# The first normalization and query projection are moved into the opening of the wide attention

## What is computed

```python
x = x + _L0_xattn_ref(_layernorm(x, axis=-1), ctx_1024, L0_xattn_ln_gamma, L0_xattn_ln_beta, L0_xattn_w_q, L0_xattn_w_kv, ...)

def _L0_xattn_ref(x, context, ln_gamma, ln_beta, w_q, w_kv, w_out, b_out, gate):
    xn = _layernorm(x, ln_gamma, ln_beta)
    q = (xn @ w_q).reshape(B, SQ, NUM_HEADS, DIM_HEAD)
    kv = context @ w_kv
    k, v = jnp.split(kv, 2, axis=-1)
    ...
    scores = jnp.einsum('bhqd,bhkd->bhqk', q * SCALE, k)
    attn = jax.nn.softmax(scores, axis=-1)
    out = jnp.einsum('bhqk,bhkd->bqhd', attn, v).reshape(B, SQ, INNER)
```

## Time and profile before

| | |
|---|---|
| median of 3 runs (lowest, highest) | 3983.5 us (3973.45, 3986.92) |
| profiled execution | 3982.38 us, its span 3980.6 us |
| busy share of the span | PE 89%, DVE 63%, ACT 58%, POOL 42% |
| mean granted TensorE clock | 0.951 |
| the part that the change touches | the first 118 us or so |

### The profile page before, as it was taken

One profiled execution on the slowest core, in us unless ns is written; L12 is line 12 of the kernel. 1 busy time (PEld: TensorE's weight loads), 2 busy tenths in 40 slices (PEclk: granted clock), 3 DMA queues, 4 the chain that ended last, 5 costly groups with the idle time before them and its releaser, 6 DMA issues. The chain is left out here.

```text
span 3980.6 us, 81241 instructions
## 1 busy us (share of the span) xinstructions
PE 3557.9 (89%) x30262; PEld 2604.8 (65%) x30262; DVE 2489.8 (63%) x3852; ACT 2289.7 (58%) x4298; POOL 1657.8 (42%) x1365
## 2 busy tenths in 40 slices
PE   6899999999999999999787976799999977679399
PEld 4687788778787788887546974455555543344398
DVE  5666666666666666664274113678788777468687
ACT  3666666666666766666252112466666666536265
POOL 0587777777777777777232002110111000014043
PEclk9999999999999999999888997799999999779699
DMA  6677767776777676665103656878787754100011
GB/s 241 253 291 285 260 257 278 275 278 249 277 276 267 249 276 240 240 240 186 42 8 132 242 216 216 191 175 168 180 168 181 137 74 65 26 15 2 20 46 43
DMA packets 231412, 723.00 MB, mean 182 GB/s; under 512 B 47324, under 2 KB 128220, under 8 KB 162140
## 3 DMA queue, kind: packets, MB, share of 16 engines
q1 hardware_dynamic: 228336, 709.44, 56.3%
q0 software_dynamic: 2688, 8.39, 0.6%
HBM read 623.47 MB, written 94.24 MB: 180 GB/s over the span
## 5 line engine op out<-in xcount | busy, mean ns | idle before, releaser
L805 POOL TENSOR_TENSOR wa_acc<-wa_acc,wa_probs 128x512 f32<-128x512 f32 x960 | 1256.9, 1309 | 460.5 <-ACT wa_probs L650 352.1
L715 DVE TENSOR_REDUCE wa_mx<-wa_ps_x 128x1 f32<-128x512 f32 x1024 | 658.6, 685 | 361.5 <-PE wa_ps_x L503 361.4
L650 ACT ACTIVATE wa_probs<-wa_ps_s 128x512 f32<-128x512 f32 x1024 | 530.4, 602 | 548.8 <-PE wa_ps_s L546 548.3
L1444 DVE TENSOR_REDUCE na_mx<-na_ps_m 128x2 f32<-128x1024 f32 x512 | 613.8, 1220 | 202.1 <-PE na_ps_m L1265 198.6
L1389 ACT ACTIVATE na_probs<-na_ps_s 128x512 f32<-128x512 f32 x1024 | 555.9, 594 | 317.5 <-PE na_ps_s L1285 315.1
L642 ACT ACTIVATE wa_ps_s<-wa_m_wide 128x512 f32<-128x512 f32 x1024 | 578.5, 614 | 0.0
L524 PE MATMUL wa_ps_o<-wa_probs,wa_values 128*64 128x256 f32 x4096 | 468.7, 381 | 0.0
L524 PEld LDWEIGHTS wa_ps_o<-wa_probs,wa_values 128*64 128x64 f32 x4096 | 285.6, 137 | 158.5 <-ACT wa_probs L650 23.9
L468 PE MATMUL wa_ps_x<-w_k_ctx,wa_w_k 128*128 128x512 f32 x1488 | 380.9, 403 | 7.7 <-DMA w_k_ctx<-ctx_split 7.3
L491 PE MATMUL wa_ps_x<-wa_w_v,w_v_ctx 128*128 128x256 f32 x2880 | 363.8, 283 | 0.1
L491 PEld LDWEIGHTS wa_ps_x<-wa_w_v,w_v_ctx 128*128 128x128 f32 x2880 | 356.9, 191 | 6.4 <-issue 0.5
(11 more groups left out here) (399 smaller groups left out, 5745.2 us busy)
## 6 DMA issues: line engine op xcount, KB each, us to landing
w_k_ctx<-ctx_split SPq DMA_DIRECT2D x248, 1024.0 KB, 6.9
w_v_ctx<-ctx_split SPq DMA_DIRECT2D x120, 1024.0 KB, 8.1
na_keys<-k_rows SPq DMA_DIRECT2D x384, 128.0 KB
na_ctx<-ctx_split SPq DMA_DIRECT2D x43, 1024.0 KB, 11.7
ctx_split<-w_stage SPq DMA_DIRECT2D x32, 1024.0 KB, 5.0
first_keep<-in_ctxT SPq DMA_DIRECT2D x32, 512.0 KB, 11.2
ge_w_b<-in_w_rows SPq DMA_DIRECT2D x8, 2048.0 KB, 7.9
k_rows<-na_k_high SPq DMA_DIRECT2D x64, 256.0 KB, 2.8
```

What stands on the lines that cost most here:

```text
L650: act.activation(probs[:, c % R:c % R + 2, h * SQ:(h + 1) * SQ], ps_s[n % BANKS][:, :].rearrange("p (c n) -> p c n", c=2), ACT.Exp).then_i ...
L715: dve.tensor_reduce(mx[:, half, h, k:k + 1], ps_x[banks[h]][:, :], AX.X, ALU.max).then_inc(m_taken, 1)
L805: pool.tensor_tensor(to[:, :], to[:, :], probs[:, c % R, :], ALU.add).then_inc(summed, 1)
L1444: dve.tensor_reduce(mx[:, half, :, k], ps_m[n % 2][:, :, :], AX.X, ALU.max).then_inc(m_taken, 1)
```

## The change

The block of the query projection disappears; its work is put into the wide block, in every engine's list.

- Loads: `x`, `ident`, the first context piece, the first weights, the second context piece, `ones`. The block still ends when `x`, `ident` and `ones` have landed. Gamma, beta and `wq` are loaded by the wide block.
- Room: `wq` lies in the last 8 chunks of `values`, the normalized rows `xn` and their transpose `xT` in `probs`, the full keys in `acc`, the queries' high and low parts on their way out in `v_ctx`. So values 6 and 7 must wait until the projection is over.
- TensorE: blocks 0 to 3 (`EARLY` = 4), then the 8 rows are turned, units 0 and 1, blocks 4 and 5, keys 6 and 7, then the 16 maxima with units 2 to 15 between them, then values 6 and 7.
- VectorE: the two normalizations, gamma and beta, units' low parts, the maxima. GpSimd takes over the low parts of the context, of the first weights and of the keys, and reads the keys from a full copy that ScalarE makes (`k_full`). ScalarE also copies the values. The units' scaled copy is gone: the high part is taken from PSUM with the scale, the low part by one `scalar_tensor_tensor`.
- SP: `store(4)` and what follows stand behind the stores of units 0 and 1 and `queries(0)`; the other units' stores stand behind `store(7)` and two context loads.

The diff, cut to its core (new semaphores, the unchanged arithmetic of `normalize`, and the passing of arguments are left out):

```diff
...
+        k_full = acc
...
+        pt, pq = [ps_o, ps_x[1]], ps_s[2:4]
...
+        UNITS = 2 * PAIRS
+        EARLY = 4
+        def unit_at(i):
+            return i + 2 if i + 2 < UNITS else None
...
+            def store_queries(n):
+                rows, cols = slice(n // 2 * P, (n // 2 + 1) * P), slice(n % 2 * 512, (n % 2 + 1) * 512)
+                sp.wait_ge(q_high_ready, n + 1)
+                sp.dma_start(q_high[rows, cols], q_stage[0][n % 2].bitcast(F32)).then_inc(q_out[n % 2], 16)
+                sp.wait_ge(q_low_ready, n + 1)
+                sp.dma_start(q_low[rows, cols], q_stage[1][n % 2].bitcast(F32)).then_inc(q_out[n % 2], 16)
+            sp.dma_start(gb[:, 0, :], gamma.partition_broadcast(P)).then_inc(affine_in, 16)
+            sp.dma_start(gb[:, 1, :], beta.partition_broadcast(P)).then_inc(affine_in, 16)
+            sp.dma_start(wq, w_q.rearrange("(k p) n -> p k n", p=P)).then_inc(wq_in, 16)
+            for k in range(EARLY):
+                fetch(k + 2)
+                store(k)
+            fetch(EARLY + 2)
+            store_queries(0)
+            store_queries(1)
+            sp.wait_ge(q_out[0], 32)
             queries(0)
-            for k in range(CG):
-                if k + 2 < CG + 2:
-                    fetch(k + 2)
-                store(k)
-                if k == 3:
+            store(EARLY)
+            fetch(EARLY + 3)
+            store(EARLY + 1)
+            fetch(EARLY + 4)
+            fetch(EARLY + 5)
+            store(CG - 2)
+            store(CG - 1)
+            key_context(CG)
+            key_context(CG + 1)
+            for n in range(2, UNITS):
+                store_queries(n)
+                if n == 3:
+                    sp.wait_ge(q_out[0], 64)
                     queries(1)
+                if n == 5:
+                    sp.wait_ge(q_out[0], 96)
+                    queries(2)
+                if n == 9:
                     key_weights(1)
-                if k == 5:
-                    key_context(CG)
-                if k == 6:
-                    key_context(CG + 1)
             key_weights(2)
-            queries(2)
+            for i in range(2):
+                sp.wait_ge(q_out[i], 16 * UNITS)
...
-                        pe.wait_ge(kl_ready, k)
+                        pe.wait_ge(kh_ready, k)
+                        pe.wait_ge(k_full_ready, k)
...
+            def project_unit(n):
+                if n >= 2:
+                    pe.wait_ge(q_high_ready, n - 1)
+                    pe.wait_ge(q_low_ready, n - 1)
+                for k in range(KD):
+                    ins = pe.matmul(pq[n % 2][:, :], wq[:, k, n // 2 * P:(n // 2 + 1) * P], xT[:, k, n % 2 * 512:(n % 2 + 1) * 512],
+                                    start=(k == 0), stop=(k == KD - 1))
+                ins.then_inc(q_done, 1)
+            def first_values(k):
+                for hb in (2 * k, 2 * k + 1):
+                    project_values(0, hb, ps_s[hb % 2])
+            for k in range(EARLY):
                 project_keys(k, ps_x[2])
-                project_values(0, 2 * k, ps_s[2 * k % BANKS])
-                if k:
-                    first_maximum(k - 1, 0)
-                project_values(0, 2 * k + 1, ps_s[(2 * k + 1) % BANKS])
-                if k:
-                    first_maximum(k - 1, 1)
-            first_maximum(CG - 1, 0)
-            first_maximum(CG - 1, 1)
+                first_values(k)
+            for t in range(NT):
+                turn_row(t)
+            pe.wait_ge(wq_in, 16)
+            pe.wait_ge(evacuated, NT)
+            project_unit(0)
+            project_unit(1)
+            for k in range(EARLY, CG):
+                project_keys(k, ps_x[2])
+                if k < CG - 2:
+                    first_values(k)
+            for i in range(2 * CG):
+                first_maximum(*divmod(i, 2))
+                if unit_at(i) is not None:
+                    project_unit(unit_at(i))
+            pe.wait_ge(q_low_ready, UNITS)
+            first_values(CG - 2)
+            first_values(CG - 1)
...
+            def root(n):
+                act.wait_ge(inv_ready, n + 1)
+                act.activation(rstd, inv, ACT.Sqrt).then_inc(root_ready, 1)
+            def first_keys(k):
+                take_keys(k, ps_x[2])
+                if k >= 2:
+                    act.wait_ge(kl_ready, k - 1)
+                act.activation(k_full[k % 2][:, :], ps_x[2][:, :], ACT.Copy).then_inc(k_full_ready, 1)
+            def first_values(k):
+                for hb in (2 * k, 2 * k + 1):
+                    act.wait_ge(vproj_done, hb + 1)
+                    act.activation(values[:, 2 * hb:2 * hb + 2, :], ps_s[hb % 2][:, :].rearrange("p (c n) -> p c n", c=2), ACT.Copy
+                                   ).then_inc(v_ready, 1)
...
+            def unit_high(n):
+                act.wait_ge(q_done, n + 1)
+                if n >= 2:
+                    act.wait_ge(q_out[n % 2], 32 * (n // 2))
+                act.activation(q_stage[0][n % 2], pq[n % 2][:, :], ACT.Copy, scale=Q_SCALE).then_inc(q_high_ready, 1)
+            act.activation(warm, ident[:, 0:1], ACT.Sqrt)
             split(0)
+            first_weights()
             split(1)
-            for k in range(CG):
-                take_keys(k, ps_x[2])
-                if k + 2 < CG:
+            root(0)
+            for k in range(EARLY):
+                first_keys(k)
+                first_values(k)
+                if k == 1:
+                    root(1)
+                split(k + 2)
+            for t in range(NT):
+                take_row(t)
+            unit_high(0)
+            unit_high(1)
+            for k in range(EARLY, CG):
+                first_keys(k)
+                if k < CG - 2:
+                    first_values(k)
                     split(k + 2)
+            for i in range(2 * CG):
+                if unit_at(i) is not None:
+                    unit_high(unit_at(i))
+            first_values(CG - 2)
+            first_values(CG - 1)
...
+            def normalize(n):
...
+            def unit_low(n):
+                dve.wait_ge(q_high_ready, n + 1)
+                dve.scalar_tensor_tensor(q_stage[1][n % 2], pq[n % 2][:, :], Q_SCALE, q_stage[0][n % 2].bitcast(F32),
+                                         ALU.mult, ALU.subtract).then_inc(q_low_ready, 1)
+            normalize(0)
+            normalize(1)
+            scale_rows()
+            unit_low(0)
+            unit_low(1)
+            for i in range(2 * CG):
+                take_maximum(0, *divmod(i, 2), (0, 1))
+                if unit_at(i) is not None:
+                    unit_low(unit_at(i))
...
+            def first_weights(n, to, land):
+                pool.wait_ge(first_high, n + 1)
+                pool.tensor_tensor(to[:, 1, :, :], land[:, :, :], to[:, 0, :, :].bitcast(F32), ALU.subtract).then_inc(first_ready, 1)
+            def split_low(n):
+                pool.wait_ge(high_ready, n + 1)
+                if n >= 2:
+                    pool.wait_ge(stored[n % 2], 16 * (n // 2))
+                pool.tensor_tensor(stage[n % 2][:, 1, :, :], land[n % 2], stage[n % 2][:, 0, :, :].bitcast(F32), ALU.subtract
+                                   ).then_inc(low_ready, 1)
+            def first_keys(k):
...
+                pool.wait_ge(k_full_ready, k + 1)
+                pool.tensor_tensor(keys_low[0][:, cols], k_full[k % 2][:, :], keys_high[0][:, cols].bitcast(F32), ALU.subtract
+                                   ).then_inc(kl_ready, 1)
+            split_low(0)
+            first_weights(0, w_k[0], k_land)
+            first_weights(1, w_v, v_land)
+            split_low(1)
             pool.wait_ge(first_ready, 2)
             load_weights(0)
+            for k in range(CG):
+                first_keys(k)
+                if k + 2 < CG:
+                    split_low(k + 2)
...
+            with nc.Block() as block:
+                @block.sync
+                def _(sp):
...
+                    sp.dma_start(x[:, :, :], x_rows).then_inc(loaded, 16)
+                    sp.dma_start(ident[:, :], a["ident"]).then_inc(loaded, 16)
+                    sp.dma_start(land0[0], a["ctxT"][0:1, :, 0:512].rearrange("o (k p) n -> p (o k) n", p=P)).then_inc(land_in[0], 16)
+                    sp.dma_start(k_land[:, :, :], w_kv[:, 0:P].rearrange("(k p) n -> p k n", p=P)).then_inc(first_in, 16)
+                    sp.dma_start(v_land[:, :, :], w_kv[:, PAIRS * P:(PAIRS + 2) * P].rearrange("(k p) n -> p k n", p=P)
+                                 ).then_inc(first_in, 16)
+                    sp.dma_start(land0[1], a["ctxT"][0:1, :, 512:1024].rearrange("o (k p) n -> p (o k) n", p=P)).then_inc(land_in[1], 16)
+                    sp.dma_start(ones[:, :], a["ones"]).then_inc(loaded, 16)
+                    sp.wait_ge(loaded, 48)
```

(20 more changed lines are left out.)

104 lines of the change are left out of this document (54 added, 50 removed).

## The result

The change makes no difference that counts, and what it makes is a loss: median 3989.9 us over 20 runs (3983.4 to 4002.7) against 3980.4 over 20 of the kernel before (3972.1 to 3987.7, and one slow execution of 6700 us, which has no part in the ratio). The ratio is 1.0024, 95% interval 1.0017 to 1.0032, so +9.6 us (6.8 to 12.7). The forecast was 3986, +2.3; the measured time is in its range and, but for the end of the interval, within the 0.3% called no change.

A forecast was written before the change was run, and what follows sets the result against it. TensorE and DMA are both nearly full in the opening's last big stage. `open_banks` at 120.9 against 117.4, less 1.2 for keys 8 and 9, gives +2.3 us on 3982.4; with 1.1 for the median, 3986, range 3972 to 3999.

The forecast's parts named there:

- the shared port: VectorE and GpSimd side by side in the opening: holding each other costed at nothing, with 5.6 us of cover.
- Blocks 0 to 3: First context blocks of the opening: TensorE starts at 17.2 us, 5.7 a block, block 3 ends at 38.0.
- rival 1: VectorE and GpSimd block each other in the opening: second root asked for at 28.5, +3 to +5 us, 3990; chance 0.12.
- Rows and first units: Eight rows behind `split(5)` at about 0.4 us each, to 45.4; units 0 and 1 take 3.45 and 1.7, to 50.7.
- Keys 6 and 7: Behind blocks 4 and 5: `store(4)` goes out at 53.8, TensorE waits 2.6 us, keys 7 end at 69.0.
- The burst: DMA traffic from 67 us: 5.5 million bytes take 15 us at 369 GB/s; unit 4 taken at 82.5, stall of 6.
- Restart and units: Units beside the maxima behind the stall: chain of 2.5 us a unit, unit 15 done at 109.6, maxima to 112.8.
- Rival 3: Faster opening: TensorE stays the bound, stores land in 5.0, chain hides; 99.5 for 117.4, so 3966; chance 0.12.
- The end: Values 6 and 7 behind the units: 6.4, copy 0.8, clock 0.8, to 120.9; keys 8 and 9 give back 1.2.
- in TensorE's terms: Count of TensorE's opening: starts 12.3 us earlier, 16 of old gaps go; new 4.5, 5, 13, 3 and 3.
- Rival 2: Units' stores in the opening land in 5.5 us, not 2.0: 3.6 a unit against 2.5, so 4001; chance 0.18.
- Rival 4: Partly faster opening: short landings -4, half the burst's stall -3, units at 2.3 -2, so 3977; chance 0.13.

The follow-up runs named there:

- E3: Changed kernel with the eight turned rows taken by ScalarE ahead of `split(5)`; ratio 1.0015 to the kernel before, landmark 125.51 for 131.63.
- E2: Changed kernel with `store(4)`, `fetch(7)` and `store(5)` issued ahead of the stores of units 0 and 1; ratio 1.0018 to the kernel before, landmark 129.26.
- E1: Changed kernel with the two 1 MB context loads issued behind unit 7's stores; ratio 1.0016 to the kernel before, landmark 131.82.
- E4: Changed kernel with the stores of units 2 to 15 issued from GpSimd's queue, `split_weights(1)` behind unit 9's; ratio 1.0028 to the kernel before, landmark 134.06.
- E5: Changed kernel with four buffers instead of two for the queries' high and low parts; 3984.1 us, landmark 129.22.
- E8: Changed kernel with E1, E2, E3, E5 and E6 together; median 3973.1 us, ratio 0.9980 to the kernel before, landmark 116.71.
- E9: E8 with the two context loads right behind `store(5)`; median 3971.8 us, ratio 0.9964 to the kernel before, landmark 111.06.
- E11: Changed kernel with the two context loads issued behind `fetch(6)`; median 3981.1 us, ratio 0.9991 to the kernel before, landmark 126.51.
- E6: Changed kernel with VectorE reducing each maximum before it makes the next unit's low part; 3990.3 us, landmark 128.79.
- E7: Changed kernel with gamma and beta left out of the first normalization, so its result lacks them; 3978.9 us, landmark 131.24.
- E10: E9 with the low parts of context blocks 6 and 7 made by VectorE; median 3971.0 us, ratio 0.9967 to the kernel before, landmark 119.64.

## Why the prediction was nearly right, and what in it was off

**The whole.** Direction, band and the order of the waits held; the sum was +2.3 for a measured +8.5 at the landmark. No rival's time came true for its reason. What was wrong are sizes, and nearly all on one side; and one term that was put at nothing, the shared port, was not nothing.

| step | forecast | measured |
|---|---|---|
| first statistics; first keys | 11.3; 17.2 | 10.94; 16.60 |
| VectorE asks for the second root | 23.2 | 29.0 |
| block 3 ends | 38.0 | 37.5 |
| norm ends; block 4's low part ends | 37.9; 39.0 | 41.2; 43.4 |
| last row taken | 45.4 | 47.1 |
| units 0 and 1 done | 50.7 | 52.97 |
| keys 6; keys 7 start | 62.9; 66.8 | 65.15; 69.22 |
| first maximum | 69.0 | 72.05 |
| `unit_high(4)` | 82.5 | 87.67 |
| a unit | 2.5 | 2.51 |
| values 6 start | 112.8 | 119.66 |
| `open_banks` | 120.9 | 127.85 |

**Blocks 0 to 3** came out on TensorE as forecast, within 0.6: GpSimd's subtraction 1024 wide, forecast 2.55 from the one 512 wide, has a median of 2.355. Beside them VectorE's norm and the low part of block 4 were 3.3 and 4.4 us late, which was covered here (see rival 1).

**Rows and first units: +2.3 us.** `split(5)` at 41.0 was seen (41.69), and E3 shows it to be the gate. But a row cost 0.61, not 0.4: turning and copying wait for each other, and the clock column is 0.65 there. I had taken the low clock for unit 0 alone. Units 0 and 1 took 5.7 for 5.15.

**Keys 6 and 7: +0.1 in the wait, +0.7 in the clock.** `store(4)` was forecast at 53.8 and issued at 56.33, late by 2.5, of which 2.3 are the units'; E2 confirms the mechanism. The second keys ran for 2.90 where 2.2 were put.

**The burst: +2.1 us.** From the first maximum to `unit_high(4)` I had 13.5 and it was 15.6. The 369 GB/s were fair (422 and 361 in two windows); the bytes weren't. Units 2 and 3 put 1.05 million of their own in before unit 4 could go, 2.7 us at 391 GB/s, and I had counted only what stood ahead of them. Over 69.2 to 87.65 us, from the start of the burst to unit 4, DMA moved 355 GB/s, that is 6.55 million bytes, the 5.5 of the forecast and these 1.05. E1, E4, E5, E8, E9 and E11 show that bytes in this stretch are the main cost, not places in a queue. The prediction's words, that unit 2's stores are "behind them" in the queue, suggest that a reordering helps; E1 and E4 refute that.

**Restart and units: +1.7 us.** 2.51 a unit was met, and E6 shows the chain to be the bound: with the low part out of it the pace is 2.35 and TensorE is never idle. So TensorE alone needs 2.35 and not the 2.17 that I put; a unit between maxima takes 1.92 from start to start of the next matmul (93.63 to 95.55), not 1.72. Rival 3, which went by 1.72, was out of reach for that too. But after 8 us of idle time the first unit took 3.21 for 1.98, a cost of the stall that I didn't put.

**The end: -0.7 us.** Keys 8 and 9 took 2.91 (-1.5, forecast -1.2); from `open_banks` to the landmark there were 3.78 us against 5.72 before, so 1.9 came back for the 1.2 forecast.

2.3 + 0.8 + 2.1 + 1.7 = 6.9 at `open_banks` (127.85 - 120.9 = 6.95), less 0.7: 6.2, which is 8.5 - 2.3.

**One side sum didn't close.** The count "in TensorE's terms" behind the sum takes 12.3 + 16 us of gain and 28.5 of loss, +0.2, where the walk has +3.5 at `open_banks`. The old gaps were 12.8 us (58.38 less 45.58 busy from 59.02 to 117.40), not 16; with 12.8 it gives +3.4. The forecast doesn't use this count.

**Rival 1's mechanism happened, and its price isn't steady.** I costed the port at nothing because medians say that the engines seldom meet, and because the second root had 5.6 us of cover. In the new opening they meet all the time, and the cover was used up. VectorE:

```profile
14.23 1.57 DVE L886 TENSOR_SCALAR wa_o_raw<-wa_o_raw 128x8 f32<-128x8 f32 x1
...
16.51 1.19 DVE L892 TENSOR_TENSOR wa_o_raw<-wa_o_raw 128x8 f32<-128x8 f32 x1
17.74 2.30 DVE L894 TENSOR_SCALAR wa_o_raw<-wa_o_raw 128x8 f32<-128x8 f32 x1
20.07 0.17 DVE L896 TENSOR_TENSOR wa_o_raw<-wa_o_raw 128x8 f32<-128x8 f32 x1
```

and GpSimd in the same microseconds:

```profile
13.42 2.35 POOL L999 TENSOR_TENSOR w_stage<-first_keep,w_stage 128x1024 fp32r<-128x1024 f32 x1 [12.97 <-ACT w_stage L701]
...
16.41 1.27 POOL L993 TENSOR_TENSOR wa_w_v<-w_v_land,wa_w_v 128x512 fp32r<-128x512 f32 x1
17.64 2.37 POOL L999 TENSOR_TENSOR w_stage<-first_keep,w_stage 128x1024 fp32r<-128x1024 f32 x1
```

Operations on 128 x 8 that take 0.17 took 1.57, 1.19 and 2.30, each ending within 0.03 us of a GpSimd instruction's end. VectorE asked for the second root at 29.0, where the forecast had 23.2 and rival 1 had 28.5. ScalarE was free at 28.3 and idled 0.72 us for it. What stood behind it, `split(3)`, could then start at 29.38; in seven other executions it still waited there 0.2 to 1.0 for its store. So in this profile the port cost at most 0.9 us, and rival 1's other terms hardly anything: GpSimd's parts of blocks 2 and 3 were longer by 0.2 us at the most, and the long one of block 4 was hidden (E7: 0.4 at the landmark). The median of 3989.9, rival 1's 3990, is no support for it.

But the record has thirteen profiled executions of this opening, and in three (E4, E8, E10) the root came 3.0 to 4.6 us after ScalarE was free, for 0.7 to 0.8 in the other ten. ScalarE's and TensorE's timeline of E10:

```profile
32.02 0.21 ACT L743 ACTIVATE wa_o_raw<-wa_o_raw 128x8 f32<-128x8 f32 x1 [4.58 <-DVE wa_o_raw L890]
...
35.79 2.90 PE L520 MATMUL wa_ps_x<-w_stage,wa_w_k 128*128 128x512 f32 x6 [4.59 <-POOL w_stage L1004]
```

In these three GpSimd began block 2's low part at 24.2 to 24.5, while VectorE's first eight scalings still ran; they took 6.6 to 7.9 us for 4.5 to 4.8. In the others it began later against VectorE, beside the last scaling or behind it. None of the edits touches this part. Block 3 then waited 2.96 to 4.59 and began at the low clock (keys 3 took 2.90 for 1.62), and ended 4 to 5 us late. In E4 `split(5)` covered it; in E8 the units ran faster behind it (3.67 for two) and the first maximum was as early as E9's; in E10 the first maximum came 3.5 us later than in E9. So the term that I put at nothing is worth between 0 and 3.5 us at the first maximum, by the execution. How often it strikes among the timed runs isn't known.

In E3, where the rows no longer wait for `split(5)`, TensorE waits 0.23 us for a row of VectorE (its row at 40.84); there it was almost free.

**Rival 2** (units' stores stay late) had its price in one place, in the burst (10.9 and 11.4 us), and not in the units that follow: the pace is 2.51, not 3.6. **Rival 3** needs the three waits to go. Even E9, with the orders rewritten, has `open_banks` at 107.27, where rival 3 has 99.5. **Rival 4** didn't happen.

## What to carry to other kernels

When work is put beside a stage that already fills the DMA engines, count every byte of the stage, the new work's own too, and then look for the idle stretch ahead of it: the same 2 MB moved forward won 5 us, moved back won nothing. Then read which instruction stands in an engine's list ahead of the one on the path; `split(5)` ahead of eight short copies cost 6 us at no gain. Put the restart at the lower clock behind each predicted stall as a term of its own. And where a wait has little cover, as the second root here, read it in several executions before you call it free.
